# A decoder layer's kernel on one core: first group's chain over three banks, mLSTM and dt matmuls padded to 128 rows, and a new order of steps by engine

## Time and profile before

| | |
|---|---|
| median of three timed runs | 1229.7 us (1226.66 to 1229.77) |
| the profiled execution: span from first to last instruction | 1224.7 us |
| its own time | not listed apart from its span |
| instructions | 27095 |
| mean granted TensorE clock | 0.939 of full |

### The profile page before, as it was taken

One profiled execution on the slowest core, in us unless ns is written; L12 is line 12 of the kernel. 1 busy time (PEld: TensorE's weight loads), 2 busy tenths in 40 slices (PEclk: granted clock), 3 DMA queues, 4 the chain that ended last, 5 costly groups with the idle time before them and its releaser, 6 DMA issues.

```text
span 1224.7 us, 27095 instructions
## 1 busy us (share of the span) xinstructions
PE 1102.9 (90%) x11540; PEld 842.8 (69%) x11540; DVE 980.0 (80%) x1219; ACT 733.8 (60%) x1728; POOL 15.2 (1%) x32
## 2 busy tenths in 40 slices
PE   8866779999999998999899989999999988998886
PEld 6743456767777676777677767777777766776775
DVE  2398978799998998999999989999988989635122
ACT  3535442776577665776587657765676656544443
POOL 4000000000000000000000000000000000000000
PEclk9777686999999999999999999999999999999998
DMA  6631523013110412041112201041104120000000
GB/s 203 204 115 58 161 93 120 36 36 106 44 62 11 131 36 70 7 134 36 36 37 82 86 17 61 17 124 45 52 11 131 35 62 1 2 2 10 2 1 10
DMA packets 52791, 76.08 MB, mean 62 GB/s; under 512 B 13696, under 2 KB 37504, under 8 KB 52672
## 3 DMA queue, kind: packets, MB, share of 16 engines
q1 hardware_dynamic: 51968, 73.81, 19.2%
q0 software_dynamic: 704, 0.56, 0.2%
HBM read 62.55 MB, written 10.75 MB: 60 GB/s over the span
## 4 chain that ended last, share of the span: by engine, by line
PE 62%; DVE 10%; ACT 8%; issue 3%; DVEq 0%; ACTq 0%
PE ps L632 7%; PE heads L642 7%; PE ps L710 6%; PE ps L703 5%; PE ps L613 5%; PE heads L663 4%; PE heads L671 4%; PE ps L535 4%; PE ps L502 3%; DVE mx L1171 3%; PE ps L559 2%; PE ps L688 2%; PE heads L688 1%; PE heads L613 1%; PE ps L690 1%
## 5 line engine op out<-in xcount | busy, mean ns | idle before, releaser
L1071 DVE TENSOR_TENSOR_SCAN ring<-dec,ring 128x1024 f32<-128x1024 f32 x128 | 292.0, 2281 | 1.7 <-ACT dec L844 1.2
L844 ACT ACTIVATE dec<-dts,a_neg 128x254 f32<-128x254 f32 x512 | 220.0, 500 | 16.8 <-DVE ring L1071 16.7
L1171 DVE TENSOR_REDUCE mx<-heads 128x16 f32<-128x2048 f32 x48 | 109.7, 2286 | 65.3 <-PE heads L663 64.7
L1080 DVE TENSOR_TENSOR ring<-ring,cs 128x1024 f32<-128x1024 f32 x128 | 156.0, 1218 | 1.9
L1064 DVE TENSOR_TENSOR ring<-dtus,bs 128x1024 f32<-128x1024 f32 x128 | 155.1, 1217 | 2.3 <-PE ps L535 1.8
L917 ACT ACTIVATE pr<-heads 128x512 f32<-128x512 f32 x192 | 99.1, 603 | 41.3 <-PE heads L676 41.3
L535 PE MATMUL ps<-ring,fold 128*32 128x256 f32 x1024 | 88.6, 416 | 26.3 <-DVE ring L1080 26.2
L710 PE MATMUL ps<-aT,wo_f 128*128 128x256 f32 x384 | 94.1, 387 | 8.0 <-DVE aT L1180 8.0
L703 PE MATMUL ps<-node,we_f 128*128 128x256 f32 x384 | 99.2, 403 | 0.0
L632 PE MATMUL ps<-node,wq_f 128*128 128x256 f32 x384 | 94.9, 390 | 3.4 <-ACT node L932 3.4
L642 PE MATMUL heads<-wv_f,node 128*128 128x256 f32 x384 | 94.1, 388 | 0.0
(11 more groups left out here) (183 smaller groups left out, 1753.5 us busy)
## 6 DMA issues: line engine op xcount, KB each, us to landing
dts<-dt_rows SPq DMA_DIRECT2D x31, 512.0 KB, 3.9
dtus<-dt_rows SPq DMA_DIRECT2D x31, 512.0 KB, 5.1
node<-in_w_edgeT SPq DMA_DIRECT2D x18, 256.0 KB, 3.1
bs<-bc_rows SPq DMA_DIRECT2D x32, 128.0 KB, 5.0
cs<-bc_rows SPq DMA_DIRECT2D x32, 128.0 KB, 5.1
dt_rows<-dt SPq DMA_DIRECT2D x32, 128.0 KB, 2.4
dt_rows<-th SPq DMA_DIRECT2D x32, 128.0 KB, 2.5
xin<-in_x SPq DMA_DIRECT2D x8, 256.0 KB, 3.1
```

The lines of the kernel that those rows point to most:

```text
L844: last = fn(dec[k % 2][:, blk, :, 1:L], dts[c % 2][:, blk, :].rearrange("p (b t) -> p b t", b=GB)[:, :, 1:L], ACT.Exp, scale=a_neg[:, c, b ...
L1071: v.tensor_tensor_scan(states, dec[k % 2][:].rearrange("p k b t -> p (k b t)"), states, 0.0, ALU.mult, ALU.add).then_inc(sig["state"], 1)
L1080: v.tensor_tensor(states[:], states[:], cs[:, q:q + 1, :].broadcast_to([P, BLKS, T]), ALU.mult).then_inc(sig["outflow"], 1)
L1171: v.tensor_reduce(mx[:].rearrange("p (h s) -> p h s", h=HPC)[:, :, 0:STEPS], heads[:].rearrange("p h (s k) -> p h s k", s=STEPS), AX.X, AL ...
```

## The change

It has four parts.

1. *First group.* The four input projections of group 0 write MA, ED, MY and MA, and PE waits only before the fourth (for the first to be read). The two halves of `u` get their Silu apart, and the x-projection starts on the first half. `a_neg` is made ahead of the x-projection's reading instead of ahead of the first decay. ACT's softplus tail of chunk 0 stands directly behind the first of the four dt readings. DVE's `setup` moves into the first layer norm, behind its bn_aggr. SP sends one of the eight `bs`/`cs` loads ahead of `dts` and seven behind.
2. *Padding.* `vaug` and `hrow` hold heads in pairs, with the ones outside (65 columns each, 130 a pair), so that the context is transposed by four full transposes instead of eight narrow matmuls; the gate matmul takes 128 output rows, with weight columns beyond its 36 (the last filled with zeros); the gate rows stand in the `zeros` tile at partitions 0 and 32, so that two full transposes replace four small ones; the dt projection takes all 128 rows of `xdn` with a `wdt` whose lower half is cleared.
3. *Order.* The `u` list is split into decays (mostly ACT), sums (PE), spreads (SP) and the rest, each with positions of its own, in quarters of a slot, and group 0 has positions apart from the later groups'.
4. *Signals* for these.

By the new positions, PE's order at the start is: warm 0 to 2, transposes, warm 3 to 8, projections 1 to 3, warm 9 to 11, fold 0, warm 12, its last bias (L449), projection 4, x-projection, mean square, warm 13 to 16, dt projection, warm 17 to 19, fold 1, warm 20, its last bias, warm 21 to 23, sums. Before it was: warm 0 to 4, transposes, projections 1 to 3, fold 0, projection 4, last bias, x-projection, mean square, warm 5, dt projection, fold 1, its last bias, warm 6 to 22, sums. DVE's first feed stands behind fold 1's last line in both. Later on PE: fold 2 follows the sum of unit 3 in both (its last bias now ahead of the sum of unit 4); fold 3 moves from behind the sum of unit 13 to ahead of that of unit 12; the sum of unit 0 of group 1 moves ahead of fold 4. On DVE, the layer norm of group 1 moves from behind the first scan to behind fold 2; mLSTM step 1 of group 0 moves ahead of the second feed of group 1.

```diff
+        IN_BANK = ((MA, ED, MY, MA), (MA,) * 4)
...
@@ sync, mamba_in
                     if i == 0:
-                        for q in range(NGRP):
-                            spread_rows(0, q)
+                        spread_row(0, 0, 0)
                 if step == 10:
                     if i == 0:
                         sp.wait_ge(sig["dt_c0"], 1)
                         first_chunk(sp, dts, dt, "dt")
+                        for q in range(NGRP):
+                            for j in range(1 if q == 0 else 0, 2):
+                                spread_row(0, q, j)
...
@@ tensor, mamba_in
-                    else:
+                    elif i:
                         after(pe, "inproj_read", i, j)
+                    elif j == 3:
+                        after(pe, "inproj_read", 0, 1)
...
-                    after(pe, "u_ready", i, 1)
+                    if i == 0:
+                        pe.wait_ge(sig["u_first"], 1)
+                    else:
+                        after(pe, "u_ready", i, 1)
                     for k in range(IC):
+                        if i == 0 and k == 2:
+                            after(pe, "u_ready", i, 1)
...
-                            last = mm(MA[:, a * T:(a + 1) * T], wdt[:, m * P:(m + 1) * P], xdn[0:R, :],
+                            last = mm(MA[:, a * T:(a + 1) * T], wdt[:, m * P:(m + 1) * P], xdn[:],
@@ tensor, mlstm
-                    for h in range(XH):
-                        r0, at = h % 2 * XD, h // 2 * T
+                    for a in range(HC):
                         for b in range(GB):
-                            last = mm(ML[i > 0][r0:r0 + XD, at + b * L:at + (b + 1) * L], vaug[:, b, h, 0:XD], ident,
-                                      start=True, stop=True, tile_position=(0, r0))
+                            last = tr(ML[i > 0][:, a * T + b * L:a * T + (b + 1) * L],
+                                      vaug[:, b, a, 1:1 + P], ident)
...
-                        last = mm(ML[i > 0][0:GROWS, 0:T], wgate[:, k, :], src[:, k % HC, :],
+                        last = mm(ML[i > 0][:, 0:T], wgate_all[:, k * GROWS:k * GROWS + P], src[:, k % HC, :],
...
-                    for j, src in enumerate((grow, gtop)):
-                        for b in range(GB):
-                            last = tr(ML[i > 0][:, (j * GB + b) * XH:(j * GB + b + 1) * XH], src[:, b * L:(b + 1) * L],
-                                      cst[0:XH, C_ID:C_ID + XH])
+                    for b in range(GB):
+                        last = tr(ML[i > 0][:, b * P:(b + 1) * P], zeros[:, b * L:(b + 1) * L], ident)
@@ scalar, mamba_in
-                if step == 4:
+                if i == 0 and step == 4:
+                    act.wait_ge(sig["conv_first"], 1)
+                    fn(u[0][:, 0:2, :], u[0][:, 0:2, :], ACT.Silu).then_inc(sig["u_first"], 1)
+                    after(act, "inproj_ps", 0, 3)
+                    fn(gate[0][:, 0:2, :].rearrange("p a b -> p (a b)"), MY[:], ACT.Silu).then_inc(sig["inproj_read"], 1)
+                if i == 0 and step == 5:
+                    after(act, "inproj_ps", 0, 4)
+                    gates = fn(gate[0][:, 2:4, :].rearrange("p a b -> p (a b)"), MA[:], ACT.Silu)
+                    gates.then_inc(sig["inproj_read"], 1)
+                    after(act, "conv_done", 0, 1)
+                    fn(u[0][:, 2:4, :], u[0][:, 2:4, :], ACT.Silu).then_inc(sig["u_ready"], 1)
...
-                        if i == 0 and c == 1:
-                            act.wait_ge(sig["dt_read"], 1)
+                        if i == 0 and c == 0:
+                            last.then_inc(sig["c0_tail"], 1)
+                            act.wait_ge(sig["c0_tail"], 1)
                             fn(th[:, 0, :], dt[:, 0, :], ACT.Abs).then_inc(sig["c0_tail"], 1)
@@ vector
                 last.then_inc(sig[f"ln_var{n}"], 1)
+                if i == 0 and n == 1:
+                    setup()
...
-            setup()
-            dve.wait_ge(sig["pool_zeros"], 1)
+            v.memset(wdt[R:P, :], 0.0)
```

More of the change, by code:

```diff
@@ L23 @@
 XP = XD + 1
+XW = 2 * XP
 NODES, EDGES = 6, 20
@@ L72 @@
 A_STEPS = [("a", "in", k) for k in range(11)]
[L73 to L74 removed]
+SPREAD_STEPS = [("u", "bc", 0), ("u", "ch", 0), ("u", "bc", 1), ("u", "ch", 1), ("u", "bc", 2), ("u", "bc", 3),
+                ("u", "ch", 2), ("u", "ch", 3)]
+DECAY_STEPS = [("u", "dec", h) for h in range(2 * UNITS)]
+UNIT_STEPS = [("u", "feed", 0)]
 for _k in range(UNITS):
[L76 removed]
     if _k >= 1:
[L78 removed]
+        UNIT_STEPS += [("u", "weigh", _k - 1)]
     if _k + 1 < UNITS:
[L80 to L88 removed]
+        UNIT_STEPS += [("u", "feed", _k + 1)]
+    UNIT_STEPS += [("u", "scan", _k)]
+    if _k >= 1 and _k % CUNITS == 0:
+        UNIT_STEPS += [("u", "gather", _k // CUNITS - 1)]
+UNIT_STEPS += [("u", "weigh", UNITS - 1), ("u", "gather", IC - 1)]
+SUM_STEPS = [("u", "add", k) for k in range(UNITS)]
 X_STEPS = [("x", "ml", k) for k in range(5)]
@@ new lines @@
+SHIFT = dict(
+    a1=[-8, 2, 2.25, 2.25, 2, 2, 2],
+    us1=[-7.75, 29, 17.5, -0.5, 3, 11.5, 26.75],
+    ua1=[0.75, 0.75, 0.75, 0.75, 0.75, 0.75, 1],
+    uv1=[1, 1, 1, 1, 1, 1, 1.25],
+    up1=[1, 0.75, 1, 1, 1, 0.5, 1.25],
+    x1=[1, 1, 1, 1, 1, 1.25, 1.25],
+)
+ORDER = [(FSLOTS * g + n, 0, g, n, step) for g in range(NG) for n, step in enumerate(F_STEPS)]
+for _rank, (_name, _steps, _groups) in enumerate((
+        ("a0", A_STEPS, (0,)),
+        ("a1", A_STEPS, range(1, NG)),
+        ("p", P_STEPS, (0,)),
+        ("ua0", DECAY_STEPS, (0,)),
+        ("ua1", DECAY_STEPS, range(1, NG)),
+        ("up0", SUM_STEPS, (0,)),
+        ("up1", SUM_STEPS, range(1, NG)),
+        ("us0", SPREAD_STEPS, (0,)),
+        ("us1", SPREAD_STEPS, range(1, NG)),
+        ("uv0", UNIT_STEPS, (0,)),
+        ("uv1", UNIT_STEPS, range(1, NG)),
+        ("w", W_STEPS, (0,)),
+        ("x0", X0_STEPS, (0,)),
+        ("x1", X_STEPS, range(1, NG)))):
+    for _k, g in enumerate(_groups):
+        _shift = SHIFT[_name][_k] if _name in SHIFT else 0
+        ORDER += [(FSLOTS * max(g - 1, 0) + at + _shift, 1 + _rank, g, n, step)
+                  for n, (step, at) in enumerate(zip(_steps, AT[_name]))]
@@ L193, in build @@
         wx = sb("wx", [P, IC, P])
-        wdt = sb("wdt", [R, I])
+        wdt = sb("wdt", [P, I])
         wout = sb("wout", [P, IC, H])
-        wgate = sb("wgate", [P, 3 * HC, GROWS])
+        wgate_all = sb("wgate", [P, 2 * HC * GROWS + P])
+        wgate = wgate_all[:, 0:3 * HC * GROWS].rearrange("p (k r) -> p k r", r=GROWS)
         a_neg = sb("a_neg", [P, IC, BLKS, NGRP])
@@ L425, in _ @@
             load(wx[:], w_x, "wx_loaded")
-            load(wdt[:], w_dt, "wx_loaded")
+            load(wdt[0:R, :], w_dt, "wx_loaded")
             load_weights(0)
             load(wout[:], w_out, "const_loaded")
-            load(wgate[:], w_gate, "const_loaded")
+            load(wgate, w_gate, "const_loaded")
             load(rowv[:], rowvecs.partition_broadcast(P), "const_loaded")
@@ L783, in mamba_in @@
                     fn(gate[p][:, 0:2, :].rearrange("p a b -> p (a b)"), MA[:], ACT.Copy).then_inc(sig["inproj_read"], 1)
-                if step == 5:
+                if i and step == 5:
                     after(act, "inproj_ps", i, 4)
```

157 lines of the change are left out of this document (85 added, 72 removed), and 7 rows, old and new, of tables (U_AT, uv0).

## The result

The changed kernel takes **1269.6 us** (median of four runs, 1261.58 to 1270.36) against 1229.7 us of the kernel before in the same comparison. The ratio is 1.031, 95% interval 1.0274 to 1.0345: slower by 3.1%. The forecast was 1223.2 us, range 1209 to 1236. The other three executions took some 8 us more, at mean granted clocks of 0.932 to 0.934 for 0.938; no trace shows where these 8 us fall.

What follows compares the result with a forecast made beforehand. The prediction saw a dependent chain set by PE's queue until the first scan, then DVE, then PE with DVE close behind. Terms +2.5 - 3 - 6 + 0 = -6.5 us took 1229.7 to 1223.2 us, range 1209 to 1236.

Steps and rivals of the forecast that it cites:

- Step 4: Steady groups, steps in new slots: no wait clearly goes, 0 us, bounds -4 and +4 over seven groups.
- Step 1: Start until the first scan: +2.5 us, first scan at 61.5 us, bounds -3 and +8.
- The reading of the chain: Start: first feed waits for L989, the fold's last line; PE's queue sets the start, not the `dts` transfer.
- the written lower bound (-3): Start until the first scan: -3 us if the clock stays high from the projection on.
- rival C: Start works as meant: clock holds, first scan 3 us earlier, DVE idle halved (-8), 1212.7 us; chance 0.20.
- Three banks win nothing: Start: projections into three banks do not bring the x-projection forward; it starts at about 33.5 us, +0.4 us.
- Step 2: First scan to first attention block, bounded by DVE: less DVE idle time, -3 us, bounds -8 and +5.
- the two waits I named: DVE before the first attention block: gate wait of 2.58 us and feed wait of 1.80 us go, together -4.4.
- late next: Before the first attention block: first mLSTM step, group 1's softplus end and fold 3 may cause waits, +1.4 us.
- Step 3: Steady groups, padding: shorter PE work, 0.9 us a group, -6 us in all, bounds -9 and 0.
- rival A: Steady groups: padding brings nothing, PE's shorter work turns into idle time, 1229.2 us; chance 0.17.
- B: Folds 1, 2 and 3 on PE at half clock delay DVE, +14.9 us, 1238.1 us; chance 0.17.

Runs made afterwards that it cites:

- experiment 3: Changed kernel with the first three decay steps of groups 1 to 7 two slots later, behind the query: 1240.6 us, ratio 1.009 to the kernel before.
- experiment 4: experiment 3 with the shifts of the chunk loads of groups 2 to 7 made even at -0.5 slots: 1236.7 us, ratio 1.0062 to the kernel before.
- experiment 1: Changed kernel with the old order of steps, all else of the change kept: 1215.5 us, ratio 0.9878 to the kernel before.
- experiment 7: Changed kernel with new positions for group 0, folds and warm-ups, old ones for groups 1 to 7: 1225.1 us, ratio 0.998 to the kernel before.
- experiment 12: Changed code with start, group 0 and group 1 in old order, groups 2 to 7 ordered as in experiment 4: 1237.9 us, ratio 1.0074.
- experiment 8: experiment 1 with all four projections of group 0 in one bank again: 1218.0 us, ratio 0.9914 to the kernel before.
- experiment 5: Kernel before with the padding alone; order, bank and transfers as before: 1217.1 us, ratio 0.991.

## Why the prediction was wrong, by its steps

**Step 4, new slots, is the one that failed.** It put them at 0, with -4 and +4 as bounds over seven groups. They cost 34.3 us there, padding's gain included. Most of the cause is shown: two slots for three decay steps 29.0 us (experiment 3), the shifted loads 4.0 (experiment 4). The profiles put it where the step is: the seven intervals take 933.1 us in the changed kernel, 911.0 in experiment 3, 901.9 in experiment 4 and 897.6 in the old order (experiment 1). The step's reasoning was "most steps shift by less than a slot or two", as if a cost were proportional to the shift. What counts is what a step passes. The decays passed the reading of the query and the norm's `rstd` on ScalarE, and their `dts` landed later than the place they were put in. The trace of before had the figures to see it: `dts` issued at 538.48, the decay at 545.63, the query reading at 544.55, and PE waiting for that query. By the 5.1 us that the load took after the change, the decay had some 2 us to spare (an estimate from these rows); the change asked for it earlier and issued the load later, and PE's chain was queued behind. For the loads the step said that they are free as long as they land ahead of their feed, and stopped there. It did not check, group by group, whether they would. Shifts of 29 and 26.75 slots put them behind the store of the attention output.

What is left after both repairs, 21.1 us to the old order, was only partly located, and its cause stays open. In the profiles, experiment 4 is 18.2 us over experiment 1: 12.6 until the first attention maximum (231.9 against 219.3) and 4.3 in the seven intervals (901.9 against 897.6). The 12.6 hold luck: experiment 3, with the same order up to that mark, reached it at 227.0. The new start costs 9.6 by itself (experiment 7, twelve runs). How the rest arises where the groups of the new order meet the start was not taken apart; experiment 12 was meant to and does not tell.

**Step 1, the start.** The reading of the chain was right: L989 decides, dt and `dts` do not. The sum was +2.5 and the profile shows -4.4. The largest term that failed is the clock's. I took 0.5 for the fourth projection because PE runs one-column matmuls ahead of it, as before; the granted clock was 1.0 there. This outcome was the written lower bound (-3) and rival C. It is no property of the order either: experiment 4 has the same order at the start, and there the clock fell at 28.1 us and the first scan came at 58.4 (in experiment 3, again the same order, at 56.5). Its PE rows, to be held against those of the changed kernel above:

```profile
27.42 2.89 PE L544 MATMUL ps<-th,win 128*128 128x256 f32 x8
31.04 3.75 PE L558 MATMUL ps<-u,wx 128*128 128x256 f32 x8 [0.73 <-issue]
```

Two executions of one order of the start, 3.8 us apart at the first scan. A sum that puts one value on the clock there is worth no more than that. But the clock is not the whole miss. With the clock as low as I took it, experiment 4's x-projection began at 31.0 for the 33.5 of my sum. It starts 0.73 us behind the end of the fourth projection, in both executions, where it was 2.24 before (30.87 to 33.11). The likely reason is that the change has `u` done in two halves and the last bias out of the way there; I had put the bias ahead of the fourth projection without taking it out behind. The first scans of the profiled executions with this code and order, 54.7 to 58.4 us, all came well before the 61.5 of the forecast. A slip of the sum belongs here too: fold 1 at full clock is 7.8 us and not 8.4, since its second pass had also been slow before (2.48 us for 1.89); it took 7.9.

"Three banks win nothing" was not tested in the new order. In the old one they were worth 2.4 us, not clearly apart (experiment 8), and most of the lead of the earlier fold was lost again. The reason I gave, fold 0's last line before the fourth projection, holds for the new order alone.

**Step 2, to the first attention block.** Forecast -3, measured +4.6 up to the first maximum (170.6 us for 165.9; the forecast's stretch ended 12 us earlier, where PE begins the block). Of the two waits I named that of 2.58 us went, and that of 1.80 shrank to 0.6. What I had as "late next" had the right kind and too small a size: ahead of the first mLSTM step DVE waits 2.79 us at 156 us where it waited 0.53. The wait for the first decay of group 1, 6.51 us at 145 us and the longest of the nine, looks like the missing term, but the next norm's `rstd` behind it waited for DVE even longer, until 151.0, and the mark came no earlier when it went (227.0 us in experiment 3). Since this mark scatters by 5 us between executions of one order (see experiment 12), the 4.6 us of one profile do not settle this step. DVE idled 26.6 us in this stretch, before 22.9.

**Step 3, padding.** Forecast -6, measured 11.1 us by the medians (experiment 5) and 5.9 in the seven intervals of the profiles (898.8 to 892.9). By itself it is 0.5 us a group where I took 0.9. PE is busy 0.9 us less a group as forecast (122.57 and 121.72, both with fill and at full clock); about half of that turned into idle time of PE, as rival A has it in its weak form. The rest in the intervals is the clock: fewer stretches at the lower level, about 1.1 us each (130.2 against 129.1). I priced instructions and not what the granted clock does in between. That the -6 came near the 5.9 of the intervals is luck.

**The rivals.** A (no gain from padding) fell: 0.991 (0.9892 to 0.9927). B (folds at half clock, slower, 1238.1) had the sign and not the cause: folds 1 and 3 ran at full clock in the profile (1.89 us a pass), and the only slow pass of fold 2 took 3.57 us for 3.65 before. C had the start of the profiled execution right and nothing else. A rival with a decay put ahead of its data was missing. The chance of slower was 0.17, nearly all of it on B, and the range ended at 1236: both came of step 4's narrow bounds, for which there was no row.

## What to carry to other kernels

When an order is changed, list for each in-order queue what every moved step now passes, and for each moved step the landing of its data: a move of three steps a group by two slots past one critical reading cost 29 us, while the changes to the code brought 13.5. Try the code and the order apart; here the changed code in the old order, with two filler matmuls a group, takes 1210.9 us, 1.4% less than before and 4.6% less than the whole change. Before crediting a PE saving of under 1% to its instructions, compare the granted clock of both traces group by group.

## What was not expected of the hardware

- The clock fell behind short waits. In the steady group shown, PE's longest wait up to the lower stretch was 1.36 us, among matmuls on 32 and 64 rows, and the granted clock was 0.52 for the next 3.4 us. Such a stretch stood there in 15 of 24 groups; with four filler instructions (1.13 us) in that wait, in none of 18.
- The same instructions can meet either clock. The changed kernel and experiment 4 have one order at the start, and the fourth projection took 1.97 us in one and 2.89 in the other, and groups of the same kernel come with and without the drop.
- An earlier arrival may be worth nothing. In experiment 8 against 1 a fold that began 4.2 us earlier brought the first scan 0.9 us; the matmuls behind it ran at the lower clock (3.76 us for 1.97).
